# Scores of the next group ahead of a K piece, a bias later in the set-up, and identity products in TensorE's pauses

## What is computed

```python
# cross-attention: every row of x against 2048 rows of context
xn, cn = layer_norm(layernorm(x), g1, b1), layer_norm(context, g2, b2)
q, k, v = xn @ Wq.T, cn @ Wk.T, cn @ Wv.T              # split into 16 heads of 32
attn = softmax(where(mask, q . k / sqrt(32), -inf))
x = x + (attn . v) @ Wo.T + bo
# self-attention
q, k, v = ln(x) @ Wq.T + bq, ln(x) @ Wk.T + bk, ln(x) @ Wv.T + bv
q, k = rope(q), rope(k)
x = x + (softmax(q . k / sqrt(32)) . v) @ Wo.T + bo
# mixture: two experts of eight for each row
rn = layernorm(ln(x)) * gamma + beta
rw, sel = top_k(softmax(rn @ gate_w.T), 2)
x = x + sum_e comb[:, e] * (gelu(rn' @ w1[e].T) @ w2[e].T)
```

## Time and profile before

| what | value |
|---|---|
| median of 3 runs | 954.24 us (953.05 to 955.04) |
| profiled execution: its time | 951.88 us |
| profiled execution: its span | 950.0 us |
| TensorE busy | 866.1 us, 91% of the span |
| VectorE, ScalarE, GpSimd busy | 71%, 56%, 41% |
| TensorE clock, mean | 0.971 of full speed |

### The profile page before, as it was taken

One profiled execution on the slowest core, in us unless ns is written; L12 is line 12 of the kernel. 1 busy time (PEld: TensorE's weight loads), 2 busy tenths in 40 slices (PEclk: granted clock), 3 DMA queues, 4 the chain that ended last, 5 costly groups with the idle time before them and its releaser, 6 DMA issues. The chain is left out here.

```text
span 950.0 us, 24410 instructions
## 1 busy us (share of the span) xinstructions
PE 866.1 (91%) x10317; PEld 607.8 (64%) x10317; DVE 679.1 (71%) x1022; ACT 528.2 (56%) x811; POOL 385.0 (41%) x294
## 2 busy tenths in 40 slices
PE   5998999999999999999999999987786499999995
PEld 2464776776766867757767757763444387776663
DVE  7765788656688555679666556676778759999893
ACT  3643454565354564454555545551567359988883
POOL 1130765345566345656444545555230032111112
PEclk9999999999999999999999999999987789999999
DMA  9354121352221232212333202206502839999993
GB/s 336 110 160 118 36 68 40 118 145 70 58 57 47 80 123 79 69 38 50 93 108 98 66 21 52 72 22 264 204 1 99 307 106 341 400 403 399 403 371 41
DMA packets 48453, 134.66 MB, mean 142 GB/s; under 512 B 9893, under 2 KB 11813, under 8 KB 44493
## 3 DMA queue, kind: packets, MB, share of 16 engines
q1 hardware_dynamic: 45354, 126.81, 39.6%
q0 software_dynamic: 2800, 6.04, 3.1%
q10 hardware_dynamic: 192, 0.26, 0.1%
HBM read 95.03 MB, written 11.31 MB: 112 GB/s over the span
## 5 line engine op out<-in xcount | busy, mean ns | idle before, releaser
L469 POOL TENSOR_TENSOR acc_pool<-acc_pool,pT 128x1024 f32<-128x1024 f32 x90 | 212.0, 2356 | 144.8 <-ACT pT L741 143.2
L741 ACT ACTIVATE pT<-ps_s 128x1024 f32<-128x1024 f32 x124 | 126.6, 1021 | 192.8 <-PE ps_s L925 192.7
L575 DVE TENSOR_REDUCE mpart<-ps_b 128x1 f32<-128x512 f32 x256 | 173.7, 685 | 74.2 <-PE ps_b L905 73.4
L889 PE MATMUL ps_a<-wv_hi,cT_hi 128*128 128x128 f16 x1024 | 183.5, 219 | 0.4 <-ACT kbias L658 0.4
L891 PE MATMUL ps_a<-wv_hi,cT_lo 128*128 128x128 f16 x1024 | 182.7, 219 | 0.0
L890 PE MATMUL ps_a<-wv_lo,cT_hi 128*128 128x128 f16 x1024 | 182.5, 219 | 0.0
L570 DVE TENSOR_TENSOR k_lo<-k_f,k_hi 128x512 f16<-128x512 f32 x64 | 77.1, 1204 | 65.9 <-ACT k_hi L714 65.9
L889 PEld LDWEIGHTS ps_a<-wv_hi,cT_hi 128*128 128x128 f16 x1024 | 99.8, 97 | 8.3 <-issue 5.9
L890 PEld LDWEIGHTS ps_a<-wv_lo,cT_hi 128*128 128x128 f16 x1024 | 100.2, 98 | 7.2
L925 PEld LDWEIGHTS ps_s<-q_stack,k_stack 101*128 101x128 f16 x992 | 72.0, 97 | 47.8 <-ACT pT L741 16.0
L925 PE MATMUL ps_s<-q_stack,k_stack 101*128 101x128 f16 x992 | 93.0, 219 | 9.8 <-ACT pT L741 8.9
(11 more groups left out here) (277 smaller groups left out, 1843.1 us busy)
## 6 DMA issues: line engine op xcount, KB each, us to landing
w_raw<-in_w SPq DMA_DIRECT2D x30, 2048.0 KB, 16.1
raw<-in_context SPq DMA_DIRECT2D x16, 1024.0 KB, 5.6
k_stack<-k_hi SPq DMA_DIRECT2D x252, 64.0 KB, 2.0
k_stack<-k_lo SPq DMA_DIRECT2D x128, 64.0 KB, 2.0
slots_in<-a_zeros SPq DMA_DIRECT2D x1, 3855.0 KB, 13.1
rows_in<-slots_in SPq DMA_DIRECT2D x15, 257.0 KB, 15.9
q_stack<-k_stack SPq DMA_DIRECT2D x12, 128.0 KB, 2.4
x_sb<-in_x SPq DMA_DIRECT2D x2, 512.0 KB, 4.3
```

Of the source, the lines that this page charges most:

```text
L469: nc.gpsimd.tensor_tensor(acc_pool[:, :], pT[:, 0, :] if p == 1 else acc_pool[:, :], pT[:, p % PT, :], ALU.add).then_inc(pool_add, 1)
L575: nc.vector.tensor_reduce(mpart[:, j, kb:kb + 1], bank_at(step)[:, :], AX.X, ALU.max).then_inc(p1_max, 1)
L741: nc.scalar.activation(pT[:, p % PT, :], scores(w, p)[:, :], ACT.Exp, scale=SM_SCALE).then_inc(exp_done, 1)
L889: nc.tensor.matmul(to, cT_hi[:, c, keys], t.wv_hi[:, c, col], start=(c == 0), stop=False)
```

## The change

It has three parts. In `window_steps` the first two score steps of the next window go ahead of the last `heavy` piece of the last pair; where a window has no such piece, the order stays. In the set-up the bias for V goes to a place after the second half of V's pieces begins, its columns ahead of `mt`; it uses banks of `ps_o`, and K and V pieces wait for two biases instead of three. In self-attention and the mixture, `keep_busy` puts float32 products of the identity with itself next to waits of TensorE; their results are not used, and the banks are overwritten by later work. No work is removed.

```diff
@@ window_steps
             if n == 3 and p == NPAIR - 1 and more:
                 steps.append(("mt", w + 1))
-                steps, av = steps + av, []
+                steps, av = steps + av + [("s", w + 1, 0, 0), ("s", w + 1, 0, 1)], []
...
-        if p == NPAIR - 1 and more:
-            steps += [("s", w + 1, 0, 0), ("s", w + 1, 0, 1)]
@@ SET_UP
-    "PE": "x0 x1 x2 x3 bias0 t0 t1 col0 q0 t2 t3 q1 t4 t5 bias2 q2 q3 col2 bias1 t6 t7 col1 v0 k0 t8 t9 k1 t10 "
-          "t11 v1 t12 t13 v2 t14 t15 k2 k3 u30 u31 p0 u32 p1 u33 p2 m00 p3 m01 p4 m02 p5 m03 p6 m10 p7 m11 p8 m12 p9 "
-          "m13 p10 m20 p11 m21 p12 m22 p13 m23 p14 p15 mt s",
-    "ACT": "x0 x1 x2 x3 fold0 bias0 t0 t1 col0 q0 t2 t3 fold1 fold2 q1 bias2 q2 t4 col2 t5 q3 bias1 t6 t7 col1 v0 "
-           "k0 t8 t9 k1 t10 t11 v1 t12 t13 t14 v2 t15 k2 k3 v3 n0 n1 n2 mt s",
+    "PE": "x0 x1 x2 x3 bias0 t0 t1 col0 q0 t2 t3 q1 bias1 t4 t5 q2 col1 q3 t6 t7 v0 k0 t8 t9 k1 t10 "
+          "t11 v1 t12 t13 v2 t14 t15 k2 k3 u30 u31 bias2 p0 u32 p1 u33 p2 m00 p3 m01 p4 m02 p5 m03 p6 m10 p7 m11 p8 m12 p9 "
+          "m13 p10 m20 p11 m21 p12 m22 p13 m23 p14 p15 col2 mt s",
+    "ACT": "x0 x1 x2 x3 fold0 bias0 t0 t1 col0 q0 t2 t3 fold1 fold2 q1 bias1 t4 t5 q2 col1 q3 t6 t7 v0 "
+           "k0 t8 t9 k1 t10 t11 v1 t12 t13 t14 v2 t15 k2 k3 v3 bias2 n0 n1 n2 col2 mt s",
@@ cross_attention
-        BIASES = (0, 2, 1)
+        BIASES = (0, 1, 2)
+
+        def bias_bank(n):
+
+            return (ps_o if n == 2 else ps_a)
@@ bias_in_a_row (and in both steps ps_a becomes bias_bank(n), on TensorE and ScalarE)
-                if n:
+                if n == 1:
                     pe.wait_ge(row_out, n)
+                if n == 2:
+                    pe.wait_ge(q_out, NG)
@@ K pieces and V pieces of window 0
-                            pe.wait_ge(bias_out, 3)
+                            pe.wait_ge(bias_out, 2)
@@ self_attention, TensorE
+            def keep_busy(to, times):
+
+                for _ in range(times):
+                    nc.tensor.matmul(to, t.ident[:, :], t.ident[:, :], start=True, stop=True)
+
             for step in STEPS:
                 a, b, c, d = stages(step)
+                drain = a is None
                 if b is not None:
                     for i in range(2):
+                        if step == 1 and i == 0:
+                            keep_busy(ps_t[0][:, 0, :], 13)
+                        if step == 2:
+                            keep_busy(ps_t[0][:, 0, :], 6)
                         pe.wait_ge(roped, 2 * b + i + 1)
...
                     for n in range(HEADS // HPG):
+                        if drain and b is not None and n >= 2:
+                            keep_busy(free_bank("o", c)[:, 0:P], 5)
                         pe.wait_ge(scaled, 2 * c + 1 + n // 2)
...
+                    if drain:
+                        keep_busy(free_bank("o", c)[:, 0:P], 4)
                     pe.wait_ge(p_out_act, 2 * c + 2)
...
                 if d is not None:
+                    if drain and not tail(step):
+                        keep_busy(free_bank("mg", d)[:, 0:P], 8)
                     pe.wait_ge(m_normed, 2 * d + (1 if tail(step) else 2))
...
                     to = free_bank("y", c)
+                    if tail(step):
+                        keep_busy(ps_p[:, 0, :], 4)
                     pe.wait_ge(o_lo, c + 1)
@@ mixture, TensorE (keep_busy as above, into ps_y[0])
+            keep_busy(11)
             pe.wait_ge(normed, 2 * EARLIER + 1)
...
+            keep_busy(4)
             pe.wait_ge(g_out, NB + 1)
...
+            keep_busy(18)
             pe.wait_ge(chose, 1)
@@ rows_picked(k)
                 pe.wait_ge(pick, k + 1)
                 if k:
                     pe.wait_ge(x_hi_s, k)
                     pe.wait_ge(x_lo_s, k)
+                else:
+                    keep_busy(4)
...
             rows_picked(0)
+            keep_busy(4)
             for k in range(TILES):
```

More of the change, by code:

```diff
@@ L652, in bias_row_out @@
                     act.wait_ge(col_mm, 1)
-                nc.scalar.activation(bias_row[n], ps_a[0][0:1, :], ACT.Copy).then_inc(row_out, 1)
+                nc.scalar.activation(bias_row[n], bias_bank(n)[0][0:1, :], ACT.Copy).then_inc(row_out, 1)
             def bias_columns_out(i):
@@ L657, in bias_columns_out @@
                 act.wait_ge(col_mm, n + 1)
-                nc.scalar.activation((qbias, kbias, vbias)[i][:, :], ps_a[1][:, NG * n:NG * (n + 1)], ACT.Copy,
+                nc.scalar.activation((qbias, kbias, vbias)[i][:, :], bias_bank(n)[1][:, NG * n:NG * (n + 1)], ACT.Copy,
                                      scale=A_SCALE if i == 2 else 1.0).then_inc(bias_out, 1)
@@ L787, in bias_in_a_row @@
                 pe.wait_ge(w_in[i], 16)
-                if n:
+                if n == 1:
                     pe.wait_ge(row_out, n)
+                if n == 2:
+                    pe.wait_ge(q_out, NG)
                 for c in range(NC):
-                    last = nc.tensor.matmul(ps_a[0][0:1, :], vectors[:, 2 + min(i, 1), c:c + 1], w_raw[i][:, c, :],
+                    last = nc.tensor.matmul(bias_bank(n)[0][0:1, :], vectors[:, 2 + min(i, 1), c:c + 1], w_raw[i][:, c, :],
                                             start=(c == 0), stop=(c == NC - 1))
@@ L800, in bias_columns @@
                 for g in range(NG):
-                    last = nc.tensor.matmul(ps_a[1][:, NG * n + g:NG * n + g + 1], bias_row[n][:, P * g:P * (g + 1)],
+                    last = nc.tensor.matmul(bias_bank(n)[1][:, NG * n + g:NG * n + g + 1], bias_row[n][:, P * g:P * (g + 1)],
                                             t.ident[0:1, 0:1], start=True, stop=True)
@@ L1857, in transposes, with keep_busy @@
                 return last
+            def keep_busy(times):
+                for _ in range(times):
+                    nc.tensor.matmul(ps_y[0][:, 0:P], t.ident[:, :], t.ident[:, :], start=True, stop=True)
+            keep_busy(11)
             pe.wait_ge(normed, 2 * EARLIER + 1)
```

## The result

The changed kernel takes 940.07 us (median of 4 runs, 934.68 to 941.36) where the kernel before took 954.64 beside it: ratio 0.984, 95% interval 0.981 to 0.986. Run again beside later experiments it took 934.41 us (932.48 to 936.25, ratio 0.979, interval 0.977 to 0.981). The forecast was 937.8, with 932 to 947 around it. The first profiled execution took 939.31 us (span 937.3, mean clock 0.989), 12.6 less than the one before (951.88).

A forecast was written before the change was run, and what follows sets the result against it. Cross-attention was bound by TensorE with waits for Exp, self-attention and routing by hand-overs, the experts by their weight stream; 2.3 + 8.2 + 1.5 + 1.7 + 1.3 + 1.4 = 16.4 us off 954.24 gave 937.8, range 932 to 947.

The forecast's parts named there:

- Scores ahead of K's last piece: Cross-attention: at fourteen window boundaries the wait of the scores for Exp goes; 8.2 us, ends 6.8 and 8.9.
- Value bias: Set-up: with V's bias later, V starts 4.5 us earlier and the first maximum comes at 70.2; 2.3 us gained.
- Clock in steps 1, 2 and 4: Self-attention: products hold TensorE's clock, so work at the lower level speeds up; 1.5, 1.7 and 1.3 us.
- VectorE's cover over the output products: Draining step of self-attention: VectorE is busy with weights, so faster output products count 0, up to 1.7 us without cover.
- In each of the thirteen pauses they fit: Self-attention and mixture: added products fit thirteen TensorE pauses within 0.05 us or better; only four behind `pick` are uncovered.
- Mixture start: Ahead of the experts: full clock gives 0.5 us on transposes and 0.9 on `rows_picked(0)`; together 1.4 us.
- the worse end that the prediction gave: Start of the mixture: a loss of 1.3 us if the clock has dropped again by the time of `pick`.
- its sign of being wrong: Profile afterwards: among others, a clock near 0.5 between 745 and 765 us less the shift would show the forecast wrong.
- The first (944.6): Rival: products don't hold the clock, or it falls elsewhere; only the order of steps gives time; 944.6 us, chance 0.20.
- The second (row of maxima): Rival: at window boundaries scores wait for the row of maxima instead of Exp; 8.2 us lost, 946.0, chance 0.08.
- The third: Rival: products at half clock outlast the pauses, 17.3 us on the path; 961.0 us, chance 0.05; decided at about three in five.

The follow-up runs named there:

- e1: The kernel before with only the next window's first scores moved ahead of K's last piece; 942.69 us against 954.05, ratio 0.990.
- e2: The kernel before with only V's bias moved in the set-up; 949.18 us, ratio 0.996.
- e5: The changed kernel with two sets of four products moved ahead of the waits they stood behind (`pick`, the output's bank); 933.29 us, ratio 0.981.
- e9: e5 with both small tables, `m_before` and `m_counting`, loaded at the start of self-attention; 934.86 us, ratio 0.979.
- e4: The changed kernel without the products, so only scores and bias moved; 940.73 us, ratio 0.986.
- e6: The changed kernel with transposes of the identity in place of the products, half as many again in each set; 937.18 us, ratio 0.985.
- e7: The changed kernel with all counts of products doubled, to 192; 944.45 us, ratio 0.992.
- e3: The kernel before with only the 96 products of the identity added, scores and bias unmoved; 951.04 us, ratio 0.996.
- e8: The changed kernel with the table `m_counting` loaded at the start of self-attention; 937.80 us, ratio 0.984.
- e10: e9 with products also in the other places where profiles showed a low clock; 930.12 us, ratio 0.975.

## Why the forecast held, point by point

The sum was 16.4 us; the medians show 14.6 and 20.8. It came out because errors of both signs met, which is partly luck: by the ratios the order gave 13.8 where 10.5 was forecast, the products 3.9 (1.2 to 6.5) where 5.9 was.

*Scores ahead of K's last piece: mechanism right, 8.2 too small.* It was summed from idle times; each boundary gave 0.74 to 0.76 us, 10.4 in e1 and 10.6 in the changed kernel, beyond the best end given (8.9). The row of maxima never became the wait.

*Value bias: 2.3 forecast, 3.7 in e2.* V starts 5.4 us earlier there (4.5 forecast) and the first maximum at 70.19 (70.2). What the step left out is the second pause for K's transfer, 1.31 us at the ninth maximum, which the longer way to the first one swallows. The columns were hidden, as forecast.

*Clock in steps 1, 2 and 4: 1.5, 1.7, 1.3 forecast; 1.0, 1.7, 1.0 in the changed kernel.* Steps 1 and 2 are read at the scores, step 4 at the copy of its values. VectorE's cover over the output products held: its result in step 4 comes 20.6 us earlier, like the copy of the values.

*"In each of the thirteen pauses they fit": this step failed.* In the last step the four products stand ahead of the wait for `a_oT_lo` in the code, but behind the claim of the bank for the output, which was last the values' bank and so waits for the same VectorE instruction. They lay open, 0.9 us; e5 shows it.

*What is late next in step 5 was missed.* With step 4 faster, TensorE is at the transposes of step 5 earlier, and ScalarE, still splitting weights, lets it wait 1.65 us, where it was 0.34. In the first profile the clock fell behind that pause and products and values ran slowly. Of 20.6 us at step 4's values, 18.2 were left at the last gate result.

*Mixture start: +1.4 forecast, -1.1 measured.* The transposes gave 0.5, as forecast. The wait for `m_counting` took 0.6: the table's load queues behind loads of weights, and in e9, with the load ahead of them, the wait is gone. It is no price of the faster self-attention: e2 and e4, which have no products, wait 0.9 and 1.1 us for the table, and e6 and e7 not at all. The four products behind `pick` took 1.1, and the 32 behind them were slow again (3.49 us), which is the worse end that the prediction gave (-1.3), and in part its sign of being wrong, a low clock between 745 and 765 us less the shift. The first expert's products ran at full clock, and as forecast that moved nothing: SP's first load stands where the scattered rows put it, 16.0 us earlier.

*Behind SP's first load* the prediction had no term. 1.4 us go in the stream of weights and 1.7 in the last tile, where the clock falls behind a pause of 2.54 us that was there before too. In the second profile and in e1, e4 to e7 and e9 the clock falls there as well; before, in e2, e3 and e8 it does not. What decides it stays open. The way from the rows' numbers to SP's loads of rows takes 14.3 to 16.7 us in the thirteen profiles, with no pattern that I found; that stays open.

*The rivals.* The first (944.6) is refuted in its first half: the products hold the clock where they stand. Its other half, falls at other places, came true in part (step 5, last tile). And the order alone (e4, 940.73) is close to the first measurement of the whole. In the changed kernel's first profile and in e3 most of what the clock gives in self-attention is lost ahead of the weights; in the second profile it is kept (14.4 us at window 15, 19.9 at SP's first load). So how much the products add to the order is not settled. The second (row of maxima) did not occur. The third needs twice the products (e7), and then costs 6.7 us against e8. Its condition was reckoned wrongly: 24.9 us of pauses and 10.5 of gain are used up by 21.1 us of products when about two in three of them run at the lower level ((24.9 + 10.5) / 21.1 - 1 = 0.68), not three in five.

The Trainium skill (TensorE: Matmul & The Clock Gate, Part 1) has the chip's look at activity run free of the program. The two profiles of the changed kernel agree: the clock fell in step 3 to 0.57 in one and stayed at 1.00 in the other. Part 4 of the same page of the Trainium skill, that transpose mode does not count as a busy TensorE in the same way, was cited with the prediction and is not borne out here: with float32 transposes of 128 x 128 the clock was 1.00 from 633 to 717 us in e6, as with products. The measurement decides.

## What to carry to other kernels

A pause of TensorE costs the idle time that the profile shows and the overlap that its neighbours lose, here a quarter more. Filling pauses keeps the clock, but the filling has to stand ahead of every wait on that path (a claim of a bank may be one), and the faster step meets what is late next. A small table is better loaded ahead of large loads than behind them in their queue. A gain ahead of a stream of transfers counted here at most as what it moved the stream's first load by.

## What the runs showed of the hardware that was not expected

- Float32 transposes, put into pauses between other work, hold the clock as well as float32 products do (e6: 1.00 in 633 to 717 us; without any filling 0.86 to 0.88).
- The same program's clock fell in step 3 in one profile and not in another, 2.8 us of difference up to the scores of step 4; a fall in window 0 or in the last tile, each there in some profiles and not in others, costs 1.5 to 1.7 us.
- Loads of 64 to 88 KB took 4.7 to 9.9 us to land while a 2 MB load was ahead of them in SP's queue, and 2.3 to 3.6 us where they were issued at the start of self-attention (e8 to e10).
